# A mixture-of-experts tail in 39 slots: thirteen slots from early counts instead of nine, by a second slot table on GpSimd

## The reference

```python
h = _layernorm(x, axis=-1) * (1 + cb) + sb
gate_logits = jnp.einsum('bsd,ed->bse', h, gate_w) + gate_b + expert_bias
top_idx = jnp.argmax(gate_logits, axis=-1)
for e in range(8):
    mask = (top_idx == e)[..., None]
    hh = jax.nn.relu(jnp.einsum('bsd,df->bsf', h, w1[e]) + b1[e])
    y = jnp.einsum('bsf,fd->bsd', hh, w2[e]) + b2[e]
    out = out + mask * y
x = x + gb * out
```

## Time and profile before

| | us |
|---|---|
| device time, median of 3 runs (lowest to highest) | 428.52 (428.21 to 428.74) |
| the profiled execution's own device time | 428.04 |
| its span | 426.3 |
| busy in the span: PE, DVE | 384.9, 347.0 |
| busy in the span: POOL, ACT | 313.0, 297.0 |
| mean granted clock of TensorE | 0.988 of full speed |

### The profile page before, as it was taken

How to read it: one execution, slowest core, us unless ns; L and a number is a source line. 1 busy time by engine, 2 the same in 40 slices (tenths; PEclk the granted TensorE clock), 3 DMA queues, 4 the chain that set the end, 5 groups by cost and what they waited for, 6 DMA issues and landing times. The chain is left out here.

```text
span 426.3 us, 10441 instructions
## 1 busy us (share of the span) xinstructions
PE 384.9 (90%) x3040; PEld 349.1 (82%) x3040; DVE 347.0 (81%) x1052; ACT 297.0 (70%) x854; POOL 313.0 (73%) x463
## 2 busy tenths in 40 slices
PE   8788989997998899698999889889999988999990
PEld 7657878897888798587889878879998977999990
DVE  6777789998879999989889997789697595788871
ACT  3776789797699988688687888898756633444430
POOL 4754894799995989679989889999956547645441
PEclk9999999999999999999999999999999999999996
DMA  8999999999920000001010110005821138888830
GB/s 239 325 334 335 334 336 332 334 335 333 312 94 2 1 2 2 0 15 37 2 52 2 50 52 1 2 2 175 312 89 50 62 106 232 263 234 216 233 102 0
DMA packets 54951, 63.29 MB, mean 148 GB/s; under 512 B 4604, under 2 KB 47996, under 8 KB 54768
## 3 DMA queue, kind: packets, MB, share of 16 engines
q1 hardware_dynamic: 50528, 55.76, 43.6%
q0 software_dynamic: 2784, 6.37, 4.2%
q10 hardware_dynamic: 1584, 0.50, 0.5%
HBM read 20.97 MB, written 42.09 MB: 148 GB/s over the span
## 5 line engine op out<-in xcount | busy, mean ns | idle before, releaser
L711 POOL TENSOR_TENSOR accb<-accb,prod 128x512 f32<-128x512 f32 x48 | 61.3, 1278 | 23.6 <-ACT accb L1082 19.6
L1975 DVE SCALAR_TENSOR_TENSOR bank<-raw,cw,bank 128x512 f32<-128x512 f32 x96 | 72.0, 750 | 2.9 <-ACT bank L1092 1.5
L744 POOL TENSOR_SCALAR lseg<-strict,av 128x128 f32<-128x128 f32 x128 | 47.8, 388 | 6.6 <-DVE av L1934 4.6
L989 POOL DMA_INDIRECT out_dram<-raw x30 | 29.2, 973 | 27.2 <-DVE raw L2420 22.7
L1515 PE MATMUL bank<-skip,cx 128*128 128x128 f32 x256 | 41.2, 283 | 7.4 <-DVE st L2023 7.0
L896 POOL DMA_INDIRECT routed_rows<-rows,rowat x32 | 32.2, 1006 | 15.7 <-issue 8.1
L1131 ACT ACTIVATE xt<-bank,dtv 128x128 f32<-128x128 f32 x128 | 39.5, 362 | 5.5 <-PE bank L1494 5.2
L1751 PE MATMUL bank<-raw 128*128 x312 | 43.3, 282 | 0.0
L1515 PEld LDWEIGHTS bank<-skip,cx 128*128 128x128 f32 x256 | 33.6, 191 | 10.3 <-DVE st L2023 9.5
L1531 PE MATMUL bank<-xt,ms 128*128 128x128 f32 x256 | 39.0, 275 | 0.0
L1508 PE MATMUL bank<-incl,lseg 128*128 128x128 f32 x256 | 38.9, 274 | 0.0
(11 more groups left out here) (273 smaller groups left out, 1141.3 us busy)
## 6 DMA issues: line engine op xcount, KB each, us to landing
routed_rows<-padrow SPq DMA_DIRECT2D x32, 1040.0 KB, 12.6
zs<-routed_rows SPq DMA_DIRECT2D x39, 130.0 KB, 3.4
xs<-in_w_dram SPq DMA_DIRECT2D x16, 258.0 KB, 3.5
hT<-in_w_dram SPq DMA_DIRECT2D x15, 258.0 KB, 3.4
zs<-in_w_dram SPq DMA_DIRECT2D x8, 258.0 KB
raw<-in_w_dram SPq DMA_DIRECT2D x1, 2048.0 KB, 10.1
xs<-in_u_dram SPq DMA_DIRECT2D x3, 512.0 KB, 8.6
routed_rows<-padrow SPq DMA_DIRECT2D x9, 130.0 KB, 3.9
```

What stands on the lines that cost most here:

```text
L711: pool.tensor_tensor(accb[:, :], accb[:, :], prod[:, :], ALU.add).then_inc(s_tapb, 1)
L744: last = pool.tensor_scalar(lseg[:, Q % LA, h, :], strict[:, d, :], av[:, b, col(d, h, t)], 1.0, ALU.mult, ALU.mult)
L1975: dve.scalar_tensor_tensor(out=acc(S, g)[:, :], in0=raw[:, g, c0:c0 + BLK], scalar=cw[:, d, g, k:k + 1], in1=acc(S, g)[:, :], op0=ALU.mult ...
```

## The change

A second table is made on POOL from the counts of five groups (`SECONDG` = 5), which guarantee `KE` = 13 full tiles. It gives slots 9 to 12, `KS` = 4 of them, that are worked on in the manner of the first phase, and the final table has 26 slots. POOL's added instructions are `second_counts` before `scatter(LASTG - 2)`, `second_table` before `scatter(LASTG - 1)`, and `taken_tiles` moves from step `LAST` to just before `scatter(LASTG)`, while a `taken_first` of the same form takes its old place. `whole`, `prefix`, `coef1`, `behind1` and `summed` are used again. SP loads slots 9 to 12 between the first and the final table. PE does them without `keep_warm` and without its own wait for the scatters. On DVE the gates of slots 0 to 5 move in front of `choose(LASTG)`, and the outputs go in three parts. POOL's `tok1` copy waits for the rows of 13 slots.

```diff
-FIRSTG = 4
+FIRSTG, SECONDG = 4, 5
 K1 = -(-(FIRSTG * BLK - NE * (P - 1)) // P)
+KE = -(-(SECONDG * BLK - NE * (P - 1)) // P)
+KS = KE - K1
...
         def sum_bank(s):
-            return turn_bank(s + 1) if s < K1 else bank[6 + s % 2]
+            return turn_bank(s + 1) if s < KE else bank[6 + s % 2]
...
             for s in range(7, K1):
                 load_w1(s, first[s])
+            sp_.wait_ge(s_firstv, 2)
+            landed(sp_, SECONDG)
+            for s in range(K1, KE):
+                at_row = first_row(s)
+                load_rows(s, at_row)
+                load_w1(s, at_row)
             sp_.wait_ge(s_tabv, 1)
...
+            def second_counts():
+
+                hold(pool, s_rt_dve, NR * (SECONDG - 1) + 5)
+                link_first(pool.tensor_tensor(whole[:, :], nextrow[:, SECONDG % 2, :], region_mid[:, :], ALU.subtract))
+                assert nf[0] == NSECOND, nf[0]
+                link_first(pool.tensor_scalar(whole[:, :], whole[:, :], 1.0 / P, ROUND, ALU.mult, ALU.add))
+                link_first(pool.tensor_scalar(first, whole[:, :], ROUND, 1.0, ALU.subtract, ALU.mult))
+                pool.tensor_scalar(whole[:, :], first, -float(P), 0.0, ALU.mult, ALU.add)
+                for k, far in enumerate((1, 2, 4)):
+                    to = prefix[:, k + 1, NE // 2:] if k < 2 else sums2[:, :]
+                    link_first(pool.tensor_tensor(to, prefix[:, k, NE // 2:], prefix[:, k, NE // 2 - far:NE // 2 + NE - far],
+                                                  ALU.add))
+                link_first(pool.tensor_tensor(taken[:, :], sums2[:, :], used[:, :], ALU.subtract))
+                link_first(pool.tensor_scalar(taken[:, :], taken[:, :], float(KS), 1.0, ALU.min, ALU.mult))
+                link_first(pool.tensor_tensor(taken[:, :], taken[:, :], used[:, :], ALU.add))
+
+            def second_table():
+
+                wide = [P, KS, NE]
+                link_first(pool.tensor_tensor(coef1[:, :], coef1[:, :], whole[:, :], ALU.add))
+                link_first(pool.tensor_tensor(behind1[:, 1, 0:KS], behind1[:, 1, 0:KS],
+                                              sums2[:, :].unsqueeze(1).broadcast_to(wide), ALU.subtract))
...
+                pool.tensor_copy(slot_r1[:, :, K1:KE], last).then_inc(s_firstv, 1)
...
             numbers(LASTG)
+            second_counts()
             scatter(LASTG - 2, 0, 3)
             half_deviation(0)
             half_deviation(1)
             scatter(LASTG - 2, 3, BT)
+            second_table()
             scatter(LASTG - 1)
+            taken_tiles()
             scatter(LASTG)
...
-            for s in range(6, K1):
-                if s + 1 < K1:
+            for s in range(6, KE):
+                if s == K1 - 1:
+                    pe.wait_ge(s_firstv, 2)
+                if s + 1 < KE:
                     hidden(s + 1)
-                    if s + 2 < K1:
+                    if s + 2 < KE:
                         turn_rows(s + 2)
                 down(s, expert_of(s))
             pe.wait_ge(s_tabv, 1)
...
-            keep_warm(bank[high_low(K1 - 2)], WARM_SCATTER)
-            landed(pe, B * NBLK)
-            keep_warm(bank[high_low(K1 - 2)], WARM_ROWS)
-            turn_rows(K1)
-            turn_rows(K1 + 1)
-            hidden(K1)
+            turn_rows(KE)
+            turn_rows(KE + 1)
+            hidden(KE)
...
             place(LASTG - 1)
             half_norm(1)
+            dve.wait_ge(s_tapb, HALO * NSTEP)
+            dve.tensor_tensor(gdiff, row[:, 1, 3, :], row[:, 0, 3, :], ALU.subtract).then_inc(s_gd, 1)
+            dve.wait_ge(s_gd, 1)
+
+            first_gates(0, 6)
             choose(LASTG)
             place(LASTG)
...
-            first_gates()
-            first_outputs(0, K1 // 2)
-            first_outputs(K1 // 2, K1)
-            rectify_high(K1)
-            for s in range(K1, NSLOT):
+            first_outputs(0, 6)
+            first_gates(6, KE)
+            first_outputs(6, 10)
+            first_outputs(10, KE)
+            rectify_high(KE)
+            for s in range(KE, NSLOT):
```

More of the change, by code:

```diff
@@ L527, in entry @@
         def entry(s, k):
[L528 removed]
+            return slot_r1[0:1, k, s:s + 1] if s < KE else slot_r[0:1, k, s - KE:s - KE + 1]
         def turn_bank(s):
@@ L620, in _ @@
                 load_w1(s, first[s])
+            sp_.wait_ge(s_firstv, 2)
[4 more added lines that the diff above has]
+                load_w1(s, at_row)
             sp_.wait_ge(s_tabv, 1)
-            first = [first_row(s) for s in range(K1, K1 + 2)]
+            first = [first_row(s) for s in range(KE, KE + 2)]
             for s in range(2):
-                load_w1(K1 + s, first[s])
+                load_w1(KE + s, first[s])
             landed(sp_, B * NBLK)
@@ L628, in _ @@
             for s in range(2):
-                load_rows(K1 + s, first[s])
-            for s in range(K1 + 2, NSLOT):
+                load_rows(KE + s, first[s])
+            for s in range(KE + 2, NSLOT):
                 at_row = first_row(s)
@@ L820, in first_table, with differences, taken_first @@
                 link_first(pool.tensor_tensor(last[:, 0], last[:, 0], slot_at1[:, :], ALU.add))
-                pool.tensor_copy(slot_r1[:, :, :], last).then_inc(s_firstv, 1)
-            def taken_tiles():
+                pool.tensor_copy(slot_r1[:, :, 0:K1], last).then_inc(s_firstv, 1)
+            def differences(of):
+                link_first(pool.tensor_tensor(gain[:, 0:NE - 1], of[:, 1:NE], of[:, 0:NE - 1], ALU.subtract))
+            def taken_first():
                 hold(pool, s_tab, NTAB0)
@@ L826, in taken_tiles @@
                 link_first(pool.tensor_scalar(used[:, :], used[:, :], float(K1), 1.0, ALU.min, ALU.mult))
-                link_first(pool.tensor_tensor(gain[:, 0:NE - 1], used[:, 1:NE], used[:, 0:NE - 1], ALU.subtract))
+                differences(used)
+                pool.tensor_scalar(coef1[:, :], gain, float(P), float(REGION), ALU.mult, ALU.add)
+                pool.tensor_tensor(behind1[:, 1, 0:KS], slot_i[:, 0:KS].unsqueeze(2).broadcast_to([P, KS, NE]),
+                                   used[:, :].unsqueeze(1).broadcast_to([P, KS, NE]), ALU.add)
@@ L965, in _ @@
                     if j == 2:
-                        taken_tiles()
+                        taken_first()
                         forward_norms(LASTG, 0, 2)
@@ L2320, in _, with link_early, first_gates, first_outputs @@
                         decay_copies(nxt)
+            ne = [0]
+            def link_early(ins):
+                ne[0] += 1
+                ins.then_inc(s_eo, 1)
+                dve.wait_ge(s_eo, ne[0])
+            def first_gates(s0, s1):
+                for s in range(s0, s1):
+                    dve.wait_ge(s_rb[s], 16)
+                link_early(dve.tensor_scalar(flag1[:, s0:s1], rr[:, s0:s1, 2 * DM:2 * DM + 1].rearrange("p s c -> p (s c)"),
+                                             float(L), None, ALU.is_ge))
+                for s in range(s0, s1):
+                    last = dve.scalar_tensor_tensor(out=gsel1[:, s, :], in0=gdiff, scalar=flag1[:, s:s + 1],
+                                                    in1=row[:, 0, 3, :], op0=ALU.mult, op1=ALU.add)
+                link_early(last)
+            def first_outputs(s0, s1):
+                dve.wait_ge(s_yo2, s1)
+                link_early(dve.tensor_tensor(ob1[:, s0:s1, :], ob1[:, s0:s1, :], gsel1[:, s0:s1, :], ALU.mult))
+                dve.tensor_tensor(ob1[:, s0:s1, :], ob1[:, s0:s1, :], rr[:, s0:s1, DM:2 * DM], ALU.add).then_inc(s_ob, s1 - s0)
             both(LASTG, 2, BT)
```

118 lines of the change are left out of this document (58 added, 60 removed).

## The result

The changed kernel takes 424.51 us (median of four runs, 421.81 to 426.09). The kernel before takes 428.63 us beside it (428.21 to 429.36). The ratio is 0.9898 with a 95% interval of 0.9851 to 0.9945, so the kernel is 4.1 us faster. The forecast was 422.3 us, 6.2 us faster, with a range of 420.4 to 424.6. The measured median is inside it by 0.1 us.

A forecast was written before the change was run, and what follows sets the result against it. PE bounds the second phase at 2.005 us a slot, behind a 6.4 us hole; 8.0 - 3.0 + 1.1 plus 0.1 for start-up gives 6.2 us off, so 422.3 us, range 420.4 to 424.6.

The forecast's parts named there:

- outputs: Rival: 13 puts before the output ring stall combine(17) 3.5 us, PE loses 1.5 to 2; 424 us, chance 0.13.
- late rows: Rival: dearer POOL instructions use up the final rows' 2.9 us cover; 423.5 to 424.5 us, chance 0.12.
- 2.33 us a slot: PE, slots 9 to 12 behind slot 8: first phase's pace, read from two neighbouring hidden blocks.
- slots run at 2.0: Rival: the four moved slots run at the second phase's pace of 2.0 us; 421.0 to 420.4, chance 0.09.
- The scatter starts some 1.0 us later: POOL, scatter behind second_counts: ten small instructions taken as 3.0 us delay its start by some 1.0 us.
- 0.6 us to spare: POOL's first half deviation ends at 331.3, DVE needs it at 331.94, so the delay is hidden.
- slower than before: Rival: second_counts delays the half norm and PE, one us per us beyond 0.6; no gain or slower, 0.06.
- The chain that ended last is 0.1 us later: POOL, scatter of group 7: starts at 342.9 against 342.77; 2.3 us later with all upper bounds.
- 0.9 us late, so it is hidden too: DVE's final table waits for taken_tiles, starts at 342.7 instead of 341.84; SP needs it only before the landing.
- DVE stalls for 1.5 us, PE 0: Output ring at combine(17): DVE stalls 1.5 us, PE's loss taken as 0, up to 1.5 at the other end.
- the later waits for rows: PE's second phase: its waits of 0.69 and 0.45 us for row loads both go, 1.1 us.
- the slots' 0.33 us each: PE, slots 9 to 12: slower first-phase pace gives back 4 x 0.33 = 1.3 us of the 6.4 us hole.

The follow-up runs named there:

- e1_again: The changed kernel run again with no edit: 425.81 us, ratio 0.9921 to the kernel before.
- e3: Changed kernel with PE reading the expert ahead of turn_rows in the first phase's loop: 424.90 us, ratio 0.9905 to the kernel before.
- e9: Changed kernel with ring of eight output buffers, early expert read, and taken_tiles before group 6's scatter with two POOL waits dropped: 422.96 us, ratio 0.9856.
- e5: Changed kernel with POOL's order alone (taken_tiles before group 6's scatter, two waits dropped): 440.37 us beside 442.42 of before, ratio 0.9951, longer series.
- e10: The changed kernel unchanged, run beside the one with all three edits: 424.25 us, ratio 0.9893 to the kernel before.
- e2: Changed kernel with eight output ring buffers instead of four: 424.69 us, ratio 0.9906 to the kernel before.
- e4: Changed kernel with six constant matmuls put back between the phases, before turn_rows(13): 425.80 us, ratio 0.9921 to the kernel before.
- e7: Changed kernel with DVE's first outputs held until group 7's last scatter is issued: 441.21 us, ratio 0.9964 to the kernel before, longer series.

## Why the prediction was right, and where its sizes were off

**The mechanism was right.** Removed hole, four slots in it, no constant matmuls needed, no clock lost, second phase bound by PE at 2.005 us: all is in the rows after. Direction and range held, the range with luck: the median is 0.1 us inside it, outside the 421.3 to 423.3 that had 0.60, and at the times that the rivals "outputs" (424) and "late rows" (423.5 to 424.5) gave. The same kernel's median in e1_again is 425.81. The size was 3.9 us of the tail (4.1, 3.2 and 5.0 by the medians of three series) against 6.2. For the profiled execution the balance is: the first turn of the second phase came 36.8 - 31.6 = 5.2 us later where the forecast had 3.0, and the second phase took 422.2 - 357.29 = 64.9 us against 426.3 - 352.83 = 73.5, so 8.6 less where the forecast had 9.2 (8.0, 1.1 and 0.1). 8.6 - 5.2 = 3.4.

**"2.33 us a slot" was too cheap.** The pair of `hidden` blocks at 340.62 and 342.95 shows no idle time before its `down`. Slots 8 to 11 show 0.22 to 0.71 us of it each, and the pace was 2.67 (2.50 and 2.60 in two more traces), which is 1.4 us over four slots (0.7 and 1.1). The rival "slots run at 2.0" named the cause by its order (turn, table read, `down`) and left its price at what one row showed. With the read in front of the turn the pace is 2.12 (e3, e9), near that rival's. Why the row before hid the read is not shown: the ranks stood ahead of it there, and PE's sequencer may have run ahead.

**"The scatter starts some 1.0 us later" and "0.6 us to spare" failed.** The ten counts were expected to take 3.0 us; they took 326.48 - 322.71 = 3.8, within the bounds. What was missing from the sum was the start of the indirect DMA behind them: 0.86 us behind a small instruction that POOL itself had waited for, 0.26 and 0.40 behind the same one when it had not (e5, e9). The half norm came 0.81 us late, PE waited 0.53, and `hidden(8)` lay 0.86 us later behind `hidden(0)` (22.60 against 21.74). This is the mechanism that the prediction had as "slower than before". Its place and its price of one us per us were right. It did not decide, but it took part. In e10, where the scatter of group 5 starts 0.6 us earlier, PE does not wait and `hidden(8)` is 0.5 us earlier (22.08). Like gaps stand before the scatters of groups 6 and 7 (0.76 and 0.84).

**"The chain that ended last is 0.1 us later" failed.** Measured from `hidden(0)`, the scatter of group 5 starts 2.5 us later (6.85 against 4.40), that of group 6 3.4 (17.66 against 14.29), that of group 7 3.2 (24.78 against 21.56), and the last one ends 4.1 us later. The first 2.5 are the forecast's 1.0, 0.8 for dearer counts and 0.7 for the gap. Of the last 0.9, 0.75 are the scatter of 1.71 us. It did not become the bound in the profiled execution only because PE was late itself. In e10 and e1 the second turn waited for rows by 1.35 and 1.15 us, in e2 and e3 the first by 1.70 and 1.50. In the last two the rows were turned 4.3 and 2.9 us behind the issue of their load, where the forecast had 2.1. The rival "late rows" had 0.12 and was there in part.

**DVE's table "0.9 us late, so it is hidden too"** was mis-sized by the same chain. DVE waited 2.54 us for `taken_tiles` and started at 344.55, not 342.7. Hidden it stayed, since the last scatter came later still.

**"DVE stalls for 1.5 us, PE 0" was mis-sized.** Of `put(13)` the forecast gave 349.7 for the first output and 366.4; it was 352.14 and 369.18, since POOL's chain was late. The landing took 373.00 - 369.18 = 3.8 us, as forecast from the earlier trace rows (3.9). The stall was 3.37, 2.79 and 1.70 us in three traces, and PE lost 0.86 and 0.70 us in the first two and nothing in the third. This is the rival "the outputs become the bound" in size (3.5 us of stall, PE 1.5 to 2 lost) but with half its price on PE.

**Right as put:** the later waits for rows (1.1 us) went, but for 0.21 us. The clock stayed at 1.00, and constant matmuls at the handover change nothing that can be measured (e4). DVE took the six gates before `choose(7)` without delay: they end at 338.32, and PE's logits, which `choose(7)` needs, at 338.64. With the three costs mended (e9) the tail is 98.2 us, against a forecast of 105.1 - 6.2 = 98.9. That is no proof of the sum, since the three edits also take out costs that the forecast had counted in, such as the slots' 0.33 us each.

**A lock behind part of it.** DVE's additions of 325.00 to 325.69 and 325.72 to 326.41 have two inputs in the on-chip memory. The small POOL instructions beside them end at 325.80 and 326.48 and take 0.62 and 0.59 us, against 0.20 of the same kind at other times. The Trainium skill, "SBUF — State Buffer", section "SBUF: two separate sides", says that such a DVE operation and a reading GpSimd operation exclude each other. These rows agree with it. That a scatter is held in the same way is what e7 shows. The prediction had named this rule and gone by the row. It is worth about 0.8 us for the counts and 0.75 for the last scatter.

With it goes a difference between traces of one and the same kernel. In after, e1, e3 and e4 the first addition starts 4.5 us behind `hidden(0)`, and POOL's next-to-last count starts inside it. In e2, e9 and e10 the addition starts 0.1 us later, just behind that count:

```profile
323.83 0.26 POOL L861 TENSOR_SCALAR taken<-taken 128x8 f32<-128x8 f32 x1
324.17 0.45 POOL L862 TENSOR_TENSOR taken<-taken,used 128x8 f32<-128x8 f32 x1
```

```profile
323.86 0.70 DVE L2151 TENSOR_TENSOR rows<-rows,row 128x512 f32<-128x512 f32 x1
```

These rows are of e10. The count takes 0.26 us and not 0.62, and the addition is hardly longer for it (0.70 against 0.69). The counts end 5.4 us behind `hidden(0)` and not 6.0, and PE does not wait for the half norm. The tails are 101.3 to 101.7 us in the first group, and 100.4 (the changed kernel) and 100.8 (e2) in the second. In e9 the scatter was earlier by its edit as well. How much of the 1.3 us comes from this is not shown, nor why the addition starts later in some executions.

**Open:** what POOL's order alone is worth, how the 2.1 us of e9 against e10 split among the three edits, why the rows' loads took 2.9 and 4.3 us from issue to turn, and what lowered the clock and made the idle times in the two longer series.

## What to carry to other kernels

When a hole on the busiest engine is filled, read what the waiting in it had hidden on every other engine. Here a register read, POOL's scatter chain and the output ring each had less cover than one row suggested, and mended one by one two of them gave 0 to 0.4 us, and all three together about 2. Put small instructions on an engine that issues indirect DMAs where it would wait anyway, and leave the last one ahead of the DMA unwaited if the DMA doesn't need it. Where one stretch varies by several us between executions, compare traces over the stretch that the change can reach, and look for a near tie between two engines before you credit an edit with the difference.

## What was unexpected of the hardware

- An indirect DMA on POOL starts 0.84 to 0.87 us behind a small instruction whose result POOL waits for, and 0.30 us behind another indirect DMA. Behind an instruction that POOL does not wait for the gap is 0.16 to 0.76 us. What stays nearly the same is the time from the end of the last instruction that was waited for, 0.85 to 1.02 us, unless the work between takes longer (0.76 is 1.02 behind such an end in after, 0.26 is 0.93 in e5).
- An indirect DMA that starts inside a DVE addition with two on-chip inputs (128x768) takes 1.70 to 1.72 us (ten traces), and 0.96 with DVE idle beside it (e7). A near tie decides the like for small instructions: one that starts 0.03 us ahead of the addition takes 0.26 us, one that starts inside it 0.62.
- The read of one number into a register on PE's queue takes 0.30 us in the median and up to 0.79 in the trace of after. It is seen as idle time of the array when only a turn of 0.27 us stands in front of it, and not when the read is moved one turn ahead (e3):

```profile
L1797 PEldq TENSOR_LOAD <-slot_r x13: 295/304/790, 320.2 to 354.6; - x13
```

(minimum, median and maximum in ns, then the first and the last start.)
